# A decoder layer on one core: packed loads, and the first half of the tokens ahead of the second on its way to the experts

## What is computed

```python
x = x + attn(_layernorm(x))                 # local attention block
x = x + xattn(ctx_1024, _layernorm(x), Wq)  # causal cross-attention
x = x + ffn(_layernorm(x))                  # router and experts

def attn(x):
    residual = x
    xi = rmsnorm(x @ down_w + down_b, norm1_w)      # 128 -> 64 channels
    # two branches of 32 channels, 8 heads of 4: windows of 10 (shift 5), of 20 (shift 10)
    xc = concat(branch(xi[:, :32]), branch(xi[:, 32:])) @ up_w + up_b
    x = residual + xc
    h = rmsnorm(x, norm2_w)
    return x + gelu(h @ ffn_w1 + ffn_b1) @ ffn_w2 + ffn_b2

def xattn(ctx, x, Wq):                     # q from x, k = v = ctx @ Wq
    scores = causal((x @ Wq) @ (ctx @ Wq).T / sqrt(128))
    return softmax(scores) @ (ctx @ Wq)

def ffn(x):                                # 8 experts, 2 taken, and a shared one
    probs = softmax(x @ router_w + router_b); weights = top2(probs)
    return shared(x) + sum_e weights[:, e] * expert_e(x)   # 128 -> 256 -> gelu -> 128
```

## Time and profile before

| | us |
|---|---|
| median of 3 runs (192.81 to 193.59) | 193.19 |
| the profiled execution | 193.48 |
| its span, first to last instruction | 191.7 |
| TensorE busy | 162.4 |
| VectorE busy | 119.6 |
| ScalarE busy | 85.4 |
| GpSimd busy | 27.7 |

### The profile page before, as it was taken

The page is one execution under the profiler, slowest core; times in us unless marked ns, Lnnn a source line. Parts: engine busy times, 40 slices in busy tenths (PEclk is TensorE's granted clock), DMA queues, the critical chain, the costliest instruction groups (busy, mean ns, idle before and its releaser), DMA issues.

```text
span 191.7 us, 3278 instructions
## 1 busy us (share of the span) xinstructions
PE 162.4 (85%) x1280; PEld 130.8 (68%) x1280; DVE 119.6 (62%) x299; ACT 85.4 (45%) x141; POOL 27.7 (14%) x37
## 2 busy tenths in 40 slices
PE   0809989999959998558877869999999999999992
PEld 0804855598848565547555648878879897979981
DVE  6184998696995989963762774655425663624423
ACT  2032261751002326007656567859690775253250
POOL 2059300007600510020132200000002000000000
PEclk9999855999997999999999999999999999999998
DMA  5999500000000000000000000000000002000001
GB/s 145 251 235 334 139 0 3 0 3 3 0 0 0 0 0 5 0 0 0 0 0 0 5 0 0 3 0 0 0 3 0 0 0 58 1 2 3 0 2 55
DMA packets 6475, 5.99 MB, mean 31 GB/s; under 512 B 1009, under 2 KB 5563, under 8 KB 6460
## 3 DMA queue, kind: packets, MB, share of 16 engines
q1 hardware_dynamic: 5260, 5.17, 10.4%
q10 hardware_dynamic: 1200, 0.62, 1.2%
HBM read 5.26 MB, written 0.52 MB: 30 GB/s over the span
## 4 chain that ended last, share of the span: by engine, by line
PE 71%; DVE 11%; ACT 6%; DMA 5%; issue 3%; SPq 2%; POOL 1%; DVEq 0%; POOLq 0%
PE ps L1081 65%; DMA wq_sb<-in_wq 5%; ACT hid L622 2%; DVE ox L847 2%; PE ps L1315 2%; DVE prod L820 2%; DVE prod L790 2%; PE ps L1107 1%; DVE prod L827 1%; DVE stat L836 1%; ACT L622 1%; ACT L609 1%; ACT L586 1%; ACT xcT L556 1%; DVE prT L915 1%
## 5 line engine op out<-in xcount | busy, mean ns | idle before, releaser
L1081 PE MATMUL ps<-moe_w_sb,hid 128*128 128x128 f32 x288 | 34.8, 276 | 0.1
L1081 PEld LDWEIGHTS ps<-moe_w_sb,hid 128*128 128x128 f32 x288 | 33.7, 192 | 1.3 <-ACT hid L622 0.5
L622 ACT ACTIVATE hid<-ps,cols_sb 128x512 f32<-128x512 f32 x36 | 24.5, 687 | 22.5 <-PE ps L1081 22.2
L990 DVE SCALAR_TENSOR_TENSOR acc<-ps,wts,acc 128x128 f32<-128x128 f32 x72 | 20.3, 344 | 20.8 <-PE ps L1081 20.6
L1081 PE MATMUL ps<-prod,half_ident 128*128 128x400 f32 x36 | 16.8, 596 | 0.8 <-ACT winT L490 0.8
L1081 PE MATMUL ps<-xf_hi,w_hi 128*128 128x512 f32 x36 | 16.2, 449 | 1.4 <-ACT hid L622 1.1
L1081 PE MATMUL ps<-prod,ident 128*128 128x200 f32 x70 | 12.7, 335 | 2.5 <-DVE prod L827 2.2
L1081 PE MATMUL ps<-xf_lo,w_hi 128*128 128x512 f32 x36 | 14.2, 395 | 0.0
L1081 PE MATMUL ps<-xf_hi,w_lo 128*128 128x512 f32 x36 | 14.1, 392 | 0.0
L1081 PEld LDWEIGHTS ps<-prod,ident 128*128 128x128 f32 x70 | 11.7, 190 | 2.9 <-DVE prod L827 2.3
L790 DVE TENSOR_TENSOR prod<-qkv 128x800 f32<-128x800 f32 (+1 forms) x16 | 13.1, 867 | 0.1
(11 more groups left out here) (140 smaller groups left out, 271.0 us busy)
## 6 DMA issues: line engine op xcount, KB each, us to landing
moe_w_sb<-in_moe_w SPq DMA_DIRECT2D x1, 1152.0 KB
xT_sb<-in_x_t SPq DMA_DIRECT2D x1, 512.0 KB, 3.9
ctxT_sb<-in_ctx_t SPq DMA_DIRECT2D x1, 512.0 KB, 7.7
out<-acc SPq DMA_DIRECT2D x8, 64.0 KB, 1.6
hid<-in_bias SPq DMA_DIRECT2D x1, 369.7 KB
x_sb<-in_x ACTq DMA_DIRECT2D x1, 320.0 KB, 7.5
ffn_w_sb<-in_ffn_w SPq DMA_DIRECT2D x2, 128.0 KB, 6.2
x_sb<-in_x ACTq DMA_DIRECT2D x1, 192.0 KB, 8.6
```

What stands on the lines that cost most here:

```text
L622: act.activation(hid[:, k % 2, c, :], ps[:, c, :], ACT.Gelu, bias=cols_sb[:, i:i + 1]).then_inc(moe_h_ready, 1)
L990: dve.scalar_tensor_tensor(acc[:, g, :], ps[:, 2 + k % 2, t * D:(t + 1) * D], wts[h][:, t, e:e + 1], acc[:, g, :], ALU.mult, ALU.add).then ...
L1081: return pe.matmul(dst, lhs, rhs, start=start, stop=stop)
```

## The change

Both the loads and the hand-written order of every queue are changed.

- Loads: x comes first on SP's queue, in a layout with one run per partition, then its transpose, one tile `consts` (identity, rows, columns), one tile `ctx` (context transposed, Wq transposed, Wq), the experts' first weights, one tile `late` (fold, causal mask, router, triangle, both ffn weights), the second weights. ScalarE's queue loads the down weights, qkv weights, the bias, the projections and up weights.
- Bias: five rows of plain float32 in place of 65 rows in split float32r; the two steps that split it are gone.
- First half: `window_product` makes no pair sums, TensorE sums four terms. Second half: `window_pairs` adds products 0, 1 and 2, 3 in one step, TensorE sums two.
- TensorE: `scores_side` moves ahead of the second part's `channels`, `v_rows` into the first half's score sums. The first half goes through its local attention, ffn and causal attention to `xf_columns(0)`; the second half's `out_columns(0, 1)`, both `out_project`, `to_tokens`, `h_columns`, `ffn_hidden`, `ffn_output` and `xl_columns` now stand between experts 0 to 5 of the first half, and its causal attention between experts 4 to 8. `value_sum(1, 1)` is cut in two.
- Around the half boundary the queue has `values(7)`, `output(0, 8)`, `xf_columns(1)`, `router_logits(1)`, then four `hidden` of the second half.
- ScalarE: `w1_high` follows `k_copy`, waits only for its own load; `router_exp` stands ahead of each half's first Gelu.
- GpSimd: `xs` is summed between the two kinds of roots; `w1_low` follows the second roots, in three cuts, without waiting for q, k, v; `rstd2_pow` is ahead of `xs_add`.
- VectorE: `xn` is computed after the first half's products; the second half's products and weighted products are spread between the first half's steps.

The diff, cut to its core:

```diff
@@ SP
+            for n, part in enumerate(PARTS):
+                sp.dma_start(x_sb[:, part, :], x[:, part, :]).then_inc(ld_x[n], 16)
+            sp.dma_start(xT_sb, x_t).then_inc(ld_xT, 16)
+            sp.dma_start(consts_sb[:], consts).then_inc(ld_vec, 16)
+            sp.dma_start(ctx_sb, ctx).then_inc(ld_ctx, 16)
+            sp.dma_start(moe_w1_sb[:], moe_w1).then_inc(ld_w1, 16)
+            sp.dma_start(late_sb[:], late).then_inc(ld_late, 16)
+            sp.dma_start(moe_w2_sb[:], moe_w2).then_inc(ld_moe, 16)
@@ GpSimd
+            pool.wait_ge(ld_vec, 16)
+            step(pool.tensor_tensor(xs[:], x_sb[:], spread(rows_sb[:, R_B2:R_B2 + D], 1, NT), ALU.add))
             for n, part in enumerate(PARTS):
                 pool.wait_ge(ss_ready, n + 1)
                 rstd(rstd1[:, part], ss[:, part], 1.0 / DI, 1e-6, rstd1_ready)
+            def w1_low():
+                pool.wait_ge(w1_high_ready, 1)
+                n = EX // W1_CUTS
+                for a in range(W1_CUTS):
+                    e = slice(a * n, (a + 1) * n)
+                    pool.tensor_tensor(w1_lo[:, e], moe_w1_sb[:, e], w1_hi[:, e].bitcast(F32),
+                                       ALU.subtract).then_inc(w1_low_ready, 1)
@@ VectorE
+            def window_pairs(b, h):
+                settle()
+                dve.tensor_tensor(prod[b][:, 0:2, :], prod[b][:, 0:2, :], prod[b][:, 2:4, :],
+                                  ALU.add).then_inc(qk_ready[b], 1)
+            products(1, 0, 0, 1, 2, 3)
+            products(0, 0, 0, 1, 2, 3)
+            xn_tiles()
             window_scores(1, 0)
             window_scores(0, 0)
+            weighted(1, 0, 0, 1, 2, 3)
             value_add(1, 0)
+            weighted(0, 0, 0, 1, 2, 3)
+            window_values(1, 0)
+            products(1, 1, 0)
             window_values(0, 0)
+            products(1, 1, 1, 2, 3)
+            window_pairs(1, 1)
             xc_add(0)
+            products(0, 1, 0)
+            xp_add(0)
+            window_scores(1, 1)
+            products(0, 1, 1, 2)
+            xp_norm(0)
+            products(0, 1, 3)
+            window_pairs(0, 1)
+            weighted(1, 1, 0, 1, 2)
+            x1_moments(0)
+            weighted(1, 1, 3)
             window_scores(0, 1)
+            x1_norm(0)
             value_add(1, 1)
             row_max(0)
...
@@ TensorE, bias
-                        mm(banks[:, a, :], bias_parts[0:k, BIAS_SEL + b * P:BIAS_SEL + (b + 1) * P],
-                           bias_parts[0:k, at:at + 400], start=False, stop=False)
+                        mm(banks[:, a, :], bias_sb[0:k, BIAS_SEL + b * P:BIAS_SEL + (b + 1) * P],
+                           bias_sb[0:k, at:at + 400], start=False, stop=False)
@@ TensorE, half boundary
             p_columns(7, 0)
+            hidden(0, 8, 1)
             p_columns(7, 1)
-            hidden(0, 6, 0)
-            hidden(0, 6, 1)
             values(7)
-            output(0, 5)
-            output(0, 6)
-            hidden(0, 7, 0)
-            hidden(0, 7, 1)
+            output(0, 8)
             xf_columns(1)
-            hidden(0, 8, 0)
-            hidden(0, 8, 1)
             router_logits(1)
-            output(0, 7)
             hidden(1, 0, 0)
-            output(0, 8)
             hidden(1, 0, 1)
             hidden(1, 1, 0)
+            hidden(1, 1, 1)
+            weight_rows(1)
+            expert_bias(1)
             output(1, 0)
...
+            for e in range(2, EX):
+                hidden(1, e, 0)
+                hidden(1, e, 1)
+                output(1, e - 1)
+            output(1, EX - 1)
```

More of the change, by code:

```diff
@@ L69, in spread, with decoder_layer @@
     return ap.broadcast_to(shape)
-def decoder_layer(nc, x, x_t, ctx_t, wq, wq_t, down_centre, identity, causal, up_w, proj_t, qkv_w,
-                  bias, fold, ffn_w1, ffn_w2, router_w, tri, cols, rows, moe_w1, moe_w2, moe_b2, out):
+def decoder_layer(nc, x, x_t, ctx, down_centre, consts, proj_up, up_w, qkv_w, bias, late, moe_w1, moe_w2,
+                  moe_b2, out):
     with ExitStack() as stack:
@@ L1008, in _ @@
-            window_values(1, 0)
-            for d in range(HD):
-                window_product(1, 1, d)
-            xc_add(0)
-            window_scores(0, 1)
-            xp_add(0)
-            for d in range(HD):
-                window_weighted(0, 1, d)
-            value_add(0, 1)
-            xp_norm(0)
-            window_scores(1, 1)
-            window_values(0, 1)
-            for d in range(HD):
-                window_weighted(1, 1, d)
+            products(1, 1, 1, 2, 3)
+            window_pairs(1, 1)
@@ L1199, in value_sum @@
                 dst = window_out(b, h).rearrange("p (d r) -> p d r", d=HD + 1)
-                for j in range(w):
-                    last = mm(dst, ident[:], src[:, :, j, :], start=(j == 0), stop=(j == w - 1))
-                last.then_inc(wv_ps[b], 1)
+                for j in range(part * w // parts, (part + 1) * w // parts):
+                    last = mm(dst, ident, src[:, :, j, :], start=(j == 0), stop=(j == w - 1))
+                if part == parts - 1:
+                    last.then_inc(wv_ps[b], 1)
             def v_rows():
@@ L1431, in _ @@
             p_columns(1, 0)
-            to_tokens(1)
+            value_sum(1, 1, 1, 2)
             p_columns(2, 0)
@@ L1437, in _ @@
             values(3)
-            h_columns(1)
-            ffn_hidden(1, 0)
-            ffn_hidden(1, 1)
+            value_sum(0, 1)
+            out_columns(1, 1)
             xf_columns(0)
-            ffn_output(1)
             router_logits(0)
```

508 lines of the change are left out of this document (226 added, 282 removed).

## The result

The changed kernel takes 220.98 us (median of 4 executions, 220.90 to 221.69) against 193.0 for the kernel before, timed beside it on the same chip; the ratio is 1.147, with a 95% interval of 1.143 to 1.151. It is 28.0 us slower. The forecast was 12 us slower, 205.0, with a range up to 211. The direction was right, the size was not. The profiled execution has a span of 219.1 us. Some kernels have slow executions, 2 to 5 us longer than their others and at a lower mean clock: the medians of the experiments leave them out, while the traces of e1 and e8 are of such ones.

A forecast was written before the change was run, and what follows sets the result against it. Behind X TensorE's queue length was taken to bound the kernel; ahead of X, a chain across engines. TensorE's end: 99.2 (X) + 88.2 (work) + 12.7 (idle) = 200.1, giving 205 us; own range 199 to 209, overall 197 to 211.

The forecast's parts named there:

- X: Time at which the first half's columns for the experts are turned; forecast 99.2 us, against 103.3 before.
- The front: Loads, normalisation and first transposes; the transposes were to start at 14.6, 3.1 us earlier than before.
- The first half's scores: First score sum at 27.6, last at 39.7, addition ending at 46.9; the lead of 3.1 becomes a lag of 0.7.
- From there to the experts: First half's value sums through ffn and norm to the turned columns; xl ready at 81.3, columns at 99.2.
- the clock falls: Rival: half clock after boundary idle time and through the score sums adds 4.7 us, giving 210; chance 0.15.
- Behind X: TensorE from the turned columns to its end; 88.2 us of work plus 12.7 us idle.
- the idle time behind X outside the boundary: Waits inside the first half's experts, such as copies behind Gelus and the second half's norm; 6.4 us, bounds 3 and 9.
- The idle time at the boundary: TensorE waits between the second half's last values and its experts, only output(0, 8) left to fill; 6.3 us, bounds 4 and 8.
- The wait for the exp and the table load: At the boundary, the second half's hidden(1, 1, 0) waits 1.4 us more because router_exp precedes all its Gelus.
- The cause it gave: Slower through idle time at the boundary of the halves and too small a lead ahead of it; chance 0.67.
- Straight through pays: Rival: VectorE hardly waits for TensorE, X falls to 85.7 and the time is a faster 191.7 us; chance 0.10.
- The packed loads bring nothing: Rival: ctx lands at 14.1 as before, the front's 3.1 us are missing, time 208.4 us; chance 0.08.

The follow-up runs named there:

- e1: Kernel before, given the changed kernel's packed loads and plain float32 bias, with the old order on TensorE, VectorE and ScalarE; 200.4 us, ratio 1.042.
- e8: Changed kernel with spare matmuls among the narrow matmuls of both halves and in four TensorE waits; two executions, 217.59 and 223.28 us.
- e4: Changed kernel with spare matmuls put into six of TensorE's waits; 219.58 us, ratio 1.142.
- e2: Kernel before with its boundary of the halves emptied, and the second half's first experts ordered, as in the changed kernel; 201.74 us, ratio 1.049.
- e3: Changed kernel with the boundary of the halves filled as in the kernel before; 221.48 us, ratio 1.151.
- e9: Same as e6 up to ffn_output(0), then the second half's local attention pulled forward and the old order from xf_columns(0); 211.96 us, ratio 1.099.
- e10: Same as e9 but with the boundary of the halves emptied as in the changed kernel; 221.38 us, ratio 1.146.
- e5: Same as e1 but with the old 65-row split float32r bias put back; 191.9 us, ratio 0.997.
- e6: Changed kernel with the bias of the kernel before (65 rows, split float32r); 219.43 us, ratio 1.139.
- e7: Same as e5 plus single spare matmuls among the first half's narrow q, k, v matmuls; 196.6 us, ratio 1.020.
- e11: Changed kernel with only v_rows moved, to between the second half's two narrow q, k, v parts; 219.77 us, ratio 1.138.

## Why the forecast was right in its sign and wrong in its size

Step by step, as the prediction put it. The timeline of TensorE in the changed kernel, from the first transposes to X:

```profile
10.71 2.93 PE L1073 MATMUL ps<-pr 128*128 128x512 f32 x4
14.99 1.25 PE L1101 MATMUL ps<-consts_sb,xi 128*32 128x128 f32 x10 [1.35 <-DVE xi L743]
...
27.74 1.58 PE L1073 MATMUL ps<-prod,half_ident 128*128 128x400 f32 x4 [0.98 <-issue]
...
48.10 2.34 PE L1073 MATMUL ps<-prod,consts_sb 128*128 128x200 f32 x6 [2.12 <-DVE prod L809]
...
64.09 1.58 PE L1073 MATMUL ps<-prod,half_ident 128*128 128x400 f32 x4 [1.66 <-DVE prod L780]
...
73.89 0.91 PE L1246 MATMUL ps<-consts_sb,sq 128*128 128x128 f32 x4 [4.75 <-DVE sq L857]
75.57 3.78 PE L1073 MATMUL ps<-hT,late_sb 128*128 128x512 f32 x4 [0.78 <-ACT hT L556]
...
89.73 1.12 PE L1266 MATMUL ps<-consts_sb,xl 128*128 128x128 f32 x4 [5.37 <-DVE xl L871]
...
108.58 1.30 PE L1073 MATMUL ps<-late_sb,ox 128*128 128x32 f32 x10 [2.24 <-DVE ox L829]
109.73 0.66 PE L1325 MATMUL ps<-consts_sb,xl 128*128 128x128 f32 x4
```

**The front: right.** The keys' matmuls start at 10.7, the transposes of xi at 15.0 (forecast 14.6), and down_b's addition takes 1.23 us beside GpSimd's xs, in the first two lines, where the same 320 elements take 0.49 in the kernel before, in the third. In e1, which sums xs later, the transposes follow the keys without a wait, at 14.31; here they wait 1.35:

```profile
10.26 1.23 DVE L732 TENSOR_TENSOR xi<-xi,consts_sb 128x320 f32<-128x320 f32 x1
```

```profile
8.80 2.35 POOL L404 TENSOR_TENSOR xs<-x_sb,consts_sb 128x1024 f32<-128x1024 f32 x1
```

```profile
12.44 0.49 DVE L749 TENSOR_TENSOR xi<-xi,rows_sb 128x320 f32<-128x320 f32 x1
```

**The first half's scores: right to 1.1 us.** First score sum 27.7 (forecast 27.6), last 40.8 (39.7), `value_add(1, 0)` ends at 47.95 (46.9). The forecast's 30 passes at 0.35 make 10.5, not its 10.2, and the traces have 0.36 from start to start for a product's pass and 0.385 for a bias pass of five rows. The lead became a lag, of 1.8 for the 0.7 forecast, and VectorE was idle for 6.04 us ahead of the first maximum.

**From there to the experts: the step that failed.** It added up durations read at the higher clock level, as if nothing followed a wait. The ten us between forecast and measurement at X build up in four places:
- "Both value sums on TensorE (20 passes, 3.65 each) end at 54.2": they took 9.74 us for the 40 passes, at the lower clock level, and ended at 57.8. The 3.65 had been read where the clock was full. Late by 3.6, of which 1.1 from the step before. No fall was forecast there.
- "Two hidden matmuls ... 72.2": `ffn_hidden` took 3.78 in place of 1.8 and ended at 79.1, with the root and the norm's product (73.15) already 4.5 late. Late by 6.9.
- "xl is ready at 81.3": it was at 89.67. The six 400-column passes between took 3.3 in place of 2.0, again at the lower level. Late by 8.4.
- "X = 99.2": 109.7. The clock was low until 94.7, and `out_columns(1, 1)`, which stands ahead of `xf_columns(0)`, waited 2.24 for VectorE's `window_values`. Late by 10.5.

Behind the lower clock stands a second mistake, of the same kind as the forecast's own argument. It priced the idle time only along the chain. TensorE's 4.75 and 5.37 us ahead of h_columns and xl_columns are in the forecast's times (xp_norm, x1's norm), but it had not asked what follows such waits. The rival "the clock falls" did, with 4.7 us and a chance of 0.15, and only at the boundary and at the score sums. By e4, spares in the five waits ahead of X, which hold the clock at 72 to 80 and 84 to 92 and shorten the fall at 43.5, bring X 6.6 us forward. Of the 4.0 that are left to the forecast 1.1 is the score sums'; the rest no run separates.

**Behind X: the sum was near, its two terms were not.** Forecast 88.2 busy and 12.7 idle, 100.9; measured 95.05 and 10.46, 105.5. The 6 us of work that had moved were priced rightly (TensorE is busy 13.0 us longer than in the kernel before, and the 13.6 us at half the clock account for up to 6.8 of them), and the idle time behind X outside the boundary was 6.3 where 6.4 was forecast, the wait for the second half's norm in it 1.61 for 1.7. The busy time is larger by the falls at 111.7 to 118.5 and 180.0 to 186.8, which the sum had at nothing. The idle time at the boundary, forecast at 6.3, was 4.2: 2.72 and 0.69 for the norm and the copy, 0.78 for the weights. The wait for the exp and the table load did not appear. ScalarE did what was forecast (load, exp, load), but TensorE was so slow that the queue of hidden matmuls just covered it:

```profile
180.10 1.28 ACT L597 ACT_TABLE_LOAD   x1
181.64 0.23 ACT L597 ACTIVATE lg<-lg 128x32 f32<-128x32 f32 x1 [0.26 <-DVE lg L929]
181.89 1.28 ACT L610 ACT_TABLE_LOAD   x1
```

```profile
178.13 0.66 PE L1325 MATMUL ps<-consts_sb,xl 128*128 128x128 f32 x4 [2.72 <-DVE xl L871]
179.47 1.46 PE L1073 MATMUL ps<-late_sb,xfT 128*128 128x8 f32 x8 [0.69 <-ACT xfT L589]
180.86 0.79 PE L1073 MATMUL ps<-xf_hi,w_hi 128*128 128x512 f32 x1
```

A pass of 512 columns takes 0.43 from start to start here and 0.23 a few us later, when the clock is back. values(7) ended at 173.6 where 160 was forecast: 10.5 from X, 3.1 from the fall and the waits behind X. From there to the end it took 41.6 where 40.1 was forecast. So TensorE's end is late by 10.5 at X and 6.9 of busy time behind it, less 2.2 of idle time that did not come: 215.2 for 200.1.

**The cause it gave: half of it.** The forecast blamed idle time at the boundary and too small a lead ahead of it. The boundary is shown to cost 9 us on the order of before (e2). But e3 shows that this is not what holds the changed kernel: with the boundary filled it is no faster. Its second half is late in any case, and e9 and e10 show that lateness at work. The forecast had the parts of that lateness, the moved work and the waits among the experts, but as terms beside the boundary's, each to be added; by the four cases they stand in for one another in part. That the sign came out right is no luck: the moved work and the idle time alone outweigh the 4.1 us of lead that it gave X. What it left out, most of it falls of the clock, is as large again (15.1 us).

**The rivals.** "Straight through pays" needed X below 87; X was 109.7, and VectorE's idle time between 28 and 99 us was nowhere near its limit of 5 us: the two waits ahead of 36.00 and 84.40 alone are 6.04 and 6.36. "The clock falls" came true, at more places than its two and for more than its 4.7 us: the stretches at the lower level are 44 us in place of 14, TensorE is busy 6.9 us longer behind X alone, and the time is over its 210. "The packed loads bring nothing" was wrong for the front (2.7 us at the transposes) and right for the end (e5, 0.997). What was left out is the float32 bias, weighed as two passes for one; in the order of before it costs about 8.5 us, most of it by the clock (e1 against e5).

In one line, against the kernel before: the order costs 27 us (e6 against e5), the bias's form perhaps 1.5 more in that order, the loads nothing that the timing shows.

## What to carry to other kernels

Work that fills a gap must be ready when the gap comes: before the second half's steps are used as filler in a later stage, look at which engine produces them and whether it has had the time, since a filler that is late becomes the chain. Price an idle time of TensorE twice, once for itself and once for the matmuls behind it at the lower clock, and take a matmul's duration from a row at each level before adding it up. An X that moved by 3 or 4 us in one trace is no effect of an edit before the clock's stretches in both traces have been laid side by side (e3, e7). Two remedies for gaps at different places (here filling the boundary, and bringing the second half forward) don't add up: measure them together as well as alone.

## What the runs showed of the hardware that was not expected

- The clock fell while TensorE was busy with narrow matmuls. In or behind passes of 33 rows it fell in every kernel of this study that has no spares among them, and in the changed kernel twice (19.6 and 43.5). With bias matmuls of five rows among the score sums it stayed at the lower level to 41.4 (e1), with 65 rows in float32r to 31.3 (e5); but e3, with five rows, has it back at 31.5. The Trainium skill, "TensorE: Matmul & The Clock Gate", section "HAM oscillation — how this bites in real kernels", speaks of waits that bring the clock down; the falls at 74.2 and 87.8, behind and in idle times of 4.75 and 5.37 us, and the one at 180, behind 2.72 and 0.69, agree with that, the one at 43.5 does not need a wait (e11).
- Idle time of about 2.2 us is not a sure sign: in the kernel before it was followed by a fall behind 55.29 and by none behind 79.21, with the same 2.16 us. Nor is the queue: e5 and e7 run the same steps at the same times from 52 us on, with idle times of 1.98 and 1.97 us ahead of the value sums, and only e7's clock falls in them.
- Spare matmuls that hold the clock at one place did not bring time: in e4 it fell later instead (176 to 189), with 0.69 and 0.33 us of idle time ahead. Why it fell there is not settled.
- GpSimd's xs holds up a VectorE step also when only one of its tensors is read from SBUF. The normalised x, `xn`, took 4.35 us in e5 with xs (19.10 to 21.48) running inside it, and 2.13 in the changed kernel with no such addition beside it. What the forecast says of steps with two inputs holds for its addition and is too narrow as a rule:

```profile
19.01 4.35 DVE L776 TENSOR_SCALAR xn<-x_sb,mv,rstd 128x128 f32<-128x128 f32 x8
```

```profile
27.83 2.13 DVE L754 TENSOR_SCALAR xn<-x_sb,mv,rstd 128x128 f32<-128x128 f32 x8
```
